# A two-layer image and token network on one core: shared score products, attention output taken by VectorE straight from PSUM, and three quarters of a normalisation moved inside the attention

## Chip, core and metric

The kernel runs on one core of a Trainium2 chip. The metric is device time in microseconds (us). TensorE (PE) multiplies matrices into PSUM, VectorE (DVE) and ScalarE (ACT) work on SBUF and PSUM, GpSimd (POOL) works on SBUF, SyncE (SP) issues the DMAs. Each engine executes its own instruction stream in order and waits on semaphores.

## What is computed

An input `x` of 4 batches x 32 images x 128 x 128 goes through two layers.

```
# layer 0, with x of [4, 32, 128, 128]; _inorm normalises one image
xn = _inorm(xa); k, q, v = three spectral convolutions of xn, 32 heads each
scores = einsum('bntk,bnsk->bnts', qf, kf) / sqrt(Hs*Ws)      # 32 x 32 for each head and batch
p_attn = softmax(scores); av = einsum('bnts,bnsk->bntk', p_attn, vf)
a   = _inorm(p(av) + xa)
m   = two spectral layers of _inorm(a)          # "layer 1" and "layer 2" of the kernel's loops
out = _inorm(m) + a ;  x = x + out
# layer 1: an image row is a token: 4 batches x 4096 tokens of 128
t = x as tokens
q, k, v = _ln_t(t) @ Wq.T, @ Wk.T, @ Wv.T
t = t + softmax(causal(q @ k.T) / sqrt(128)) @ v
t = t + expert layer of _ln_t(t) (64 experts, top 8 tokens each)
```

In the kernel a batch of the second layer is 32 tiles of 128 tokens (4096 tokens), 4 batches, 128 tiles in all.

## The kernel before

**Score products (layer 0).** The scores of the image attention are computed in the frequency domain, as a complex product with three real products in place of four. A product is a tile of 128 modes x (16 heads x 128 images): DVE multiplies modes of the images (`XLT`) by a weight of each head (`CT`) into one of four buffers `ZP`, PE contracts it into the score banks with 4 matmuls (8 in the trace). There are 2 halves of the heads x 5 mode tiles x 3 products = 30, in `score_products` (L1037), all on DVE, both inputs in SBUF. PE's matmul is L1344. Afterwards DVE adds and subtracts a maximum (L1711 to L1715), ACT takes the exponential (L1469), DVE goes on. ACT's stream is in order: ahead of the exponential stand 128 row-wise activations of the image (L1466), and a load of its function table.

**Value products.** 36 x 3 products, DVE (L981, one input in PSUM) with POOL beside it (L993).

**End of layer 0.** `_inorm(m) + a`, in 32 groups of 4 images. Of each four groups ACT normalises three (L1545) and DVE one (L1911); POOL adds the result to `U` (`x1_ready`, L1183); DVE takes the statistics for the token normalisation (L1773). Then all 128 coefficients are computed (`row_moments`, `token_norm`; ready at L773, `norm_ready`), and the attention starts. The weights of the token layer are prepared ahead of it by DVE (`fold_weights`, L741 to L755) and PE (L373 to L375).

**The attention of layer 1** is written out in slots, one for each of 288 units (72 a batch; a unit is two key tiles of 128 by a query group of up to 512). In slot s PE computes the scores of unit s (`scores`, 2 x 3 matmuls), weighs the values with unit s-2 (`weigh`, 2 x 3 matmuls), and computes up to three pieces of the row maxima for a later group (`top_scores`, L433). ACT takes two exponentials per unit (L654 in f32, L657 in f16; `ex_ev`, `hi_ev`), DVE the difference of the two (L827, both inputs in SBUF; `lo_ev`) and the maxima (L807). Score banks are double buffered, the f16 halves threefold.

At most one job a slot uses the spare bank, PSUM bank 7: `kt` (turn tokens), `qp` (project queries), `m` (turn maxima) and `out` (apply the value weights to the sums of a finished group; two halves a group, in adjacent slots mostly). Before a job PE waits in `spare_bank` until the job ahead of it has emptied the bank (`kt_ev`, `ql_ev`, `ml_ev`, `os_ev`). `attention_plan` sets jobs to slots by due times.

An `out` job is finished by three engines: ACT copies the bank into `OTM` (L690, `os_ev`), DVE takes the reciprocals of the sums (L839), POOL scales (2 x L622) and adds to `U` (L625, `or_ready`), DVE takes statistics three slots later (L846). POOL also prepares the tokens of the next batch, 8 chunks a batch (`prep_slot`, L609 to L612), and DVE splits them (`split_low`, L798).

## Time and profile before

| | before |
|---|---|
| median of 3 runs | 2064.22 us (2062.46 to 2067.7) |
| profiled execution, own time | 2063.2 us |
| its span in the trace | 2061.3 us |
| PE / DVE / ACT / POOL busy | 84% / 76% / 51% / 24% |
| score products | 124.25 to 190.4 us |
| end of layer 0 to coefficients ready | 799.15 to 855.66 us |
| attention with its start | 855.7 to about 1819.7 us |

The span runs from the first to the last instruction; times in the trace count from its start. A share of busy time is a mean over stages with different limits. A wait is read from an instruction's idle time and its releaser.

### The profile page before, as it was taken

How to read it: one execution, taken by the hardware profiler on the slowest of the kernel's cores; microseconds unless marked ns; L12 is line 12 of the kernel's file. 1: busy time of each engine (PE TensorE's matmuls, PEld its weight loads, DVE VectorE, ACT ScalarE, POOL GpSimd, SP SyncE). 2: the span in 40 equal slices, each digit the busy share in tenths (PEclk: the TensorE clock that was granted, in tenths of full speed). 3: DMA queues.
4: the chain of work that ended last, by engine and by line, in shares of the span. 5: the costliest groups of instructions: out<-in, count | busy, mean ns of one | idle time of the engine just before them, and what ended most of it. 6: DMA issues, size and time to landing. Idle time of an engine off the chain costs nothing.

```text
span 2061.3 us, 31131 instructions
## 1 busy us (share of the span) xinstructions
PE 1729.3 (84%) x11530; PEld 1076.7 (52%) x11530; DVE 1569.2 (76%) x3012; ACT 1059.8 (51%) x1632; POOL 491.8 (24%) x591
## 2 busy tenths in 40 slices
PE   8765777899789993189999899998999999966767
PEld 8631222699789893044444444454444544434535
DVE  5789999538766689789887888778886888578345
ACT  5396000133545246356677667776667777772110
POOL 2200666100190073524200541125200311000000
PEclk9886999999899996589999999999999999998878
DMA  6550353000000050001000110001000000030686
GB/s 171 203 148 11 85 127 76 1 1 1 1 1 1 1 170 1 3 8 24 11 1 1 21 21 1 1 1 32 11 1 1 1 1 1 1 123 1 216 306 172
DMA packets 113683, 101.00 MB, mean 49 GB/s; under 512 B 39168, under 2 KB 91776, under 8 KB 112992
## 3 DMA queue, kind: packets, MB, share of 16 engines
q1 hardware_dynamic: 113536, 99.02, 17.0%
q8 instruction: 95, 1.56, 0.3%
q14 instruction: 52, 0.43, 0.1%
HBM read 80.27 MB, written 12.44 MB: 45 GB/s over the span
## 4 chain that ended last, share of the span: by engine, by line
PE 62%; DVE 23%; issue 6%; ACT 3%; DMA 3%; POOL 2%; SPq 1%; POOLq 0%; DVEq 0%; ACTq 0%
PE PS L451 5%; PE PS L453 5%; PE PS L452 5%; PE PS L470 5%; PE PS L472 5%; PE PS L471 5%; PE PS L1269 4%; DVE U L981 4%; PE PS L1278 4%; PE PS L433 4%; DVE U L1037 3%; PE PS L1196 3%; PE PS L1402 3%; DMA V<-in_L_ffn_weight 3%; DVE ST L1773 2%
## 5 line engine op out<-in xcount | busy, mean ns | idle before, releaser
L827 DVE TENSOR_TENSOR DB<-Z 128x1024 f16<-128x1024 f32 (+2 forms) x288 | 335.2, 1164 | 117.6 <-ACT Z L657 69.0
L654 ACT ACTIVATE Z<-PS,MI 128x1024 f32<-128x1024 f32 (+2 forms) x288 | 300.5, 1043 | 240.8 <-PE PS L453 206.8
L807 DVE TENSOR_REDUCE MI<-PS 128x1 f32<-128x512 f32 (+2 forms) x576 | 357.5, 639 | 47.7 <-PE PS L433 31.3
L657 ACT ACTIVATE Z<-PS,MI 128x1024 f16<-128x1024 f32 (+2 forms) x288 | 298.7, 1037 | 0.0
L622 POOL TENSOR_SCALAR Z<-Z,MI 128x128 f32<-128x128 f32 x128 | 89.1, 707 | 699.6 <-DVE MI L839 699.6
L981 DVE TENSOR_TENSOR U<-A,PS 128x1408 f32<-128x1408 f32 x108 | 166.1, 1615 | 1.2 <-PE PS L1368 1.2
L993 POOL TENSOR_TENSOR U<-A,U 128x1408 f32<-128x1408 f32 x36 | 113.9, 3196 | 192.0 <-DVE MI L1734 137.7
L1374 PE MATMUL PS<-U 128*32 128x352 f32 x1152 | 110.7, 480 | 0.1
L470 PE MATMUL PS<-Z,A 128*128 128x512 f16 (+3 forms) x288 | 104.0, 361 | 4.3 <-ACT CST L665 4.0
L470 PE MATMUL PS<-Z,V 128*128 128x512 f16 (+3 forms) x288 | 104.0, 361 | 3.8 <-ACT CST L665 3.6
L1269 PE MATMUL PS<-CST,A 128*66 128x128 f32 x768 | 104.8, 281 | 0.5 <-DVE A L1769 0.5
L451 PE MATMUL PS<-V 128*128 128x512 f16 (+3 forms) x288 | 104.6, 363 | 0.0
L453 PE MATMUL PS<-V 128*128 128x512 f16 (+3 forms) x288 | 104.5, 363 | 0.0
L452 PE MATMUL PS<-V 128*128 128x512 f16 (+3 forms) x288 | 104.5, 363 | 0.0
L451 PE MATMUL PS<-A,V 128*128 128x512 f16 (+3 forms) x288 | 104.2, 362 | 0.0
L453 PE MATMUL PS<-A,V 128*128 128x512 f16 (+3 forms) x288 | 104.0, 361 | 0.0
L471 PE MATMUL PS<-DB,V 128*128 128x512 f16 (+3 forms) x288 | 104.0, 361 | 0.0
L452 PE MATMUL PS<-A,V 128*128 128x512 f16 (+3 forms) x288 | 104.0, 361 | 0.0
L471 PE MATMUL PS<-DB,A 128*128 128x512 f16 (+3 forms) x288 | 104.0, 361 | 0.0
L472 PE MATMUL PS<-Z,V 128*128 128x512 f16 (+3 forms) x288 | 103.9, 361 | 0.0
L472 PE MATMUL PS<-Z,A 128*128 128x512 f16 (+3 forms) x288 | 103.9, 361 | 0.0
L1278 PE MATMUL PS<-CST,DB 66*128 66x128 f32 x768 | 100.6, 275 | 0.1
(412 smaller groups left out, 3710.2 us busy)
## 6 DMA issues: line engine op xcount, KB each, us to landing
V<-in_L_ffn_weight SPq DMA_DIRECT2D x32, 1024.0 KB, 7.6
A<-x_planes SPq DMA_DIRECT2D x24, 528.0 KB, 9.7
U<-in_x SPq DMA_DIRECT2D x16, 512.0 KB, 3.8
V<-in_x SPq DMA_DIRECT2D x4, 2048.0 KB, 13.9
Z<-in_x SPq DMA_DIRECT2D x16, 512.0 KB, 3.9
out<-U SPq DMA_DIRECT2D x16, 512.0 KB, 5.0
U<-e_planes SPq DMA_DIRECT2D x48, 132.0 KB, 7.2
x_planes<-Z SPq DMA_DIRECT2D x2, 1056.0 KB, 8.0
```

Source lines behind the costliest of these rows:

```text
L451: pe.matmul(o, kh[:, ks], qh[:, qs], start=True, stop=False)
L452: pe.matmul(o, kh[:, ks], ql[:, qs], start=False, stop=False)
L453: mm = pe.matmul(o, kl[:, ks], qh[:, qs], start=False, stop=k < 4 * g)
L470: pe.matmul(o, xh[:, k, :], ph, start=k == 0, stop=False)
L471: pe.matmul(o, xh[:, k, :], pl, start=False, stop=False)
L472: mm = pe.matmul(o, xl[:, k, :], ph, start=False, stop=k == 4 * g + 3)
L654: act.activation(EX32[u % 2][:, 0:w], s, ACT.Exp, scale=SCALE / (QUP * KUP), bias=pb).then_inc(sem("ex_ev"), 1)
L657: act.activation(EHI[u % 3][:, 0:w], s, ACT.Exp, scale=SCALE / (QUP * KUP), bias=pb).then_inc(sem("hi_ev"), 1)
L807: dve.tensor_reduce(bm[:, g % 2, t, k:k + 1], PS[:, 4 + chunk_no[c] % 2, 0:w], AX.X, ALU.max).then_inc(sem("ch_ev"), 1)
L827: dve.tensor_tensor(ELO[u % 3][:, 0:w], EX32[u % 2][:, 0:w], EHI[u % 3][:, 0:w], ALU.subtract).then_inc(sem("lo_ev"), 1)
L981: dve.tensor_tensor(YB[d % 2][:, :, q, :], XR[:, r % 2, :, q, :], PS[:, 6 + i % 2, 0:MR].unsqueeze(1).broadcast_to([128, B, MR]), ALU.mult ...
L1269: mm = pe.matmul(PS[0:66, ROW_BANKS[k % 3], 128 * j:128 * j + 128], A_modes[:, :, 4 * k + j], cst["ih"], start=True, stop=True)
```

## The change

1. **Score products.** Of the three products the third goes to POOL (`pool_score_products`, 10 products, two buffers `ZPP` in `Z`), the other two stay on DVE (20). DVE now reads the modes from PSUM, where PE's transposes have put them (`turned`), and the sum of real and imaginary part is accumulated there by 10 more matmuls in place of two DVE adds. The products no longer wait for the Gram matrix except the third (its buffer is read by it).
2. **Attention output.** DVE finishes an `out` job alone from PSUM: reciprocals and two `scalar_tensor_tensor` that scale and add to `U`. ACT's copy, POOL's three instructions and `OTM` are gone. `os_ev` is now given by DVE.
3. **End of layer 0.** Only groups 0 to 7 (batch 0) are normalised ahead of the attention, 6 by ACT and 2 by DVE. Groups 8 to 31 are done in the slots 2, 4, ..., 48 of batch 0: even groups by ACT, odd by POOL, all added by POOL. DVE takes their statistics in the slots 3 to 17 (batch 1), 60 to 67 (batch 2), 132 to 139 (batch 3), and the coefficients of a batch are computed in the slots 20, 70, 142 (`NORM_AT`) and the one behind each. The preparation of batch 1 and its `qp` jobs move later (slots 22 to 43 and 52 to 62), and buffers change places so that the images are not overwritten.
4. **Weights of the token layer** are prepared inside the inverse loop of layer 2: `fold_weights` at step 6, PE's part at step 12 (`token_weights`), `take_weights` at step 18.

```diff
+STATS_AT = {1: 3, 2: 60, 3: 132}
+NORM_AT = {1: 20, 2: 70, 3: 142}
...
         def prep_slot(b, c):
-            return UB * (b - 1) + 3 + 3 * c if b else slots.start + 3 * (c // 2)
+            return UB * (b - 1) + (3, 22)[b == 1] + 3 * c if b else slots.start + 3 * (c // 2)
+
+        def image_slot(g):
+            return 2 * (g - 7)
+
+        def by_pool(g):
+            return g >= 8 and g % 2 == 1
+
+        def by_dve(g):
+            return g in (2, 5)
...
-            def add_out(job):
-                _, b, g, h = job
-                n = kind_no[job]
-                pool.wait_ge(sem("os_ev"), n + 1)
-                pool.wait_ge(sem("rd_ready"), n + 1)
-                x = OTM[n % 2][:, :, 0:128]
-                for j in range(2):
-                    ins = pool.tensor_scalar(x[:, j], x[:, j], rd[:, n % 2, j:j + 1], None, ALU.mult)
-                pool_steps.later(ins)
-                u = U[:, NT * b + 4 * g + 2 * h:NT * b + 4 * g + 2 * h + 2, :]
-                pool.tensor_tensor(u, u, x, ALU.add).then_inc(sem("or_ready"), 1)
...
-                        act.activation(OTM[n % 2], PS[:, 7, :].rearrange("p (j d) -> p j d", j=2)[:, :, 0:130], ACT.Copy).then_inc(sem("os_ev"), 1)
...
+                for g in range(8, NIM):
+                    if image_slot(g) == s and not by_pool(g):
+                        last_norm(act, g)
+                for b in range(1, B):
+                    if NORM_AT[b] == s:
+                        root_tokens(b)
...
                 elif kind == "out":
                     n = kind_no[job]
-                    dve.wait_ge(sem("os_ev"), n + 1)
-                    dve.reciprocal(rd[:, n % 2, :], OTM[n % 2][:, :, 128]).then_inc(sem("rd_ready"), 1)
+                    dve.wait_ge(sem("out_mm"), n + 1)
+                    later(dve.reciprocal(rd[:, n % 2, :], PS[:, 7, 128:385:256]))
+                    for j in range(2):
+                        u = U[:, NT * b + 4 * x + 2 * y + j, :]
+                        ins = dve.scalar_tensor_tensor(u, PS[:, 7, 256 * j:256 * j + 128], rd[:, n % 2, j:j + 1], u, ALU.mult, ALU.add)
+                    ins.then_inc(sem("os_ev"), 1)
...
+                for b in range(1, B):
+                    if 0 <= s - STATS_AT[b] < 16 and (s - STATS_AT[b]) % (2 if b == 1 else 1) == 0 and (b == 1 or s - STATS_AT[b] < 8):
+                        g = 8 * b + (s - STATS_AT[b]) // (2 if b == 1 else 1)
+                        dve.wait_ge(sem("x1_ready"), g + 1)
+                        image_stats(U, g).then_inc(sem("st_ready"), 1)
+                    if NORM_AT[b] == s:
+                        dve.wait_ge(sem("st_ready"), 8 * b)
+                        token_variance(slice(NT * b, NT * b + NT))
+                    if NORM_AT[b] + 1 == s:
+                        batch_norm(b)
...
-            eng.tensor_tensor(ZP[z % 4][0:w], XLT[0:w, xc, k, :].unsqueeze(1).broadcast_to([w, 16, N]),
-                              CT[0:w, wc, k, 16 * h:16 * h + 16].unsqueeze(2).broadcast_to([w, 16, N]),
+            dve.tensor_tensor(ZP[n % 4][0:w], turned(2 - c, k, w).unsqueeze(1).broadcast_to([w, 16, N]),
+                              CT[0:w, c, k, 16 * h:16 * h + 16].unsqueeze(2).broadcast_to([w, 16, N]),
                               ALU.mult).then_inc(sem("zp_dve"), 1)
+
+        def pool_score_products(pool, i):
+            h, k = divmod(i, NLC)
+            w = min(128, ML - 128 * k)
+            if i >= 2:
+                pool.wait_ge(sem("s_mm"), 3 * (i - 1))
+            pool.tensor_tensor(ZPP[i % 2][0:w], XLT[0:w, 0, k, :].unsqueeze(1).broadcast_to([w, 16, N]),
+                               CT[0:w, 2, k, 16 * h:16 * h + 16].unsqueeze(2).broadcast_to([w, 16, N]),
+                               ALU.mult).then_inc(sem("zp_pool"), 1)
...
+            pool.wait_ge(sem("xlt_ev"), 1)
+            pool.wait_ge(sem("x_out"), 48)
+            for i in range(2 * NLC):
+                pool_score_products(pool, i)
```

VectorE in the slots 75 and 76, the start of batch 1, before: `L827` is the difference of the halves, `L807` a row maximum, `L839` the reciprocal of an `out` job, which waits for ACT's copy (`os_ev`), `L798` the split of a prepared chunk, which waits for POOL (`xh_pool`).

```order
L807 TENSOR_REDUCE MI<-PS 128x1 [waits ch_mm]
L839 RECIPROCAL MI<-Z 128x2 [waits os_ev]
L807 TENSOR_REDUCE MI<-PS 128x1 [waits ch_mm]
L827 TENSOR_TENSOR DB<-Z 128x1024 [waits pv_mm,hi_ev,ex_ev]
L807 TENSOR_REDUCE MI<-PS 128x1 [waits ch_mm]
L839 RECIPROCAL MI<-Z 128x2 [waits os_ev]
L807 TENSOR_REDUCE MI<-PS 128x1 [waits ch_mm] x2
L798 TENSOR_TENSOR V<-Z,V 128x512 [waits xh_pool]
L827 TENSOR_TENSOR DB<-Z 128x896 [waits pv_mm,hi_ev,ex_ev]
```

The same place of VectorE after the change (`L857` is the maximum, `L877` the difference, `L889` and `L892` the `out` job, `L848` the split):

```order
L857 TENSOR_REDUCE MI<-PS 128x1 [waits ch_mm]
L889 RECIPROCAL MI<-PS 128x2 [waits out_mm]
L892 SCALAR_TENSOR_TENSOR U<-PS,MI,U 128x128 [waits dve_step]
L892 SCALAR_TENSOR_TENSOR U<-PS,MI,U 128x128
L857 TENSOR_REDUCE MI<-PS 128x1 [waits ch_mm]
L877 TENSOR_TENSOR DB<-Z 128x1024 [waits pv_mm,hi_ev,ex_ev]
L857 TENSOR_REDUCE MI<-PS 128x1 [waits ch_mm]
L889 RECIPROCAL MI<-PS 128x2 [waits out_mm]
L892 SCALAR_TENSOR_TENSOR U<-PS,MI,U 128x128 [waits dve_step]
L892 SCALAR_TENSOR_TENSOR U<-PS,MI,U 128x128
L857 TENSOR_REDUCE MI<-PS 128x1 [waits ch_mm] x2
L848 TENSOR_TENSOR A<-Z,A 128x512 [waits xh_pool]
```

One reciprocal a job has become a reciprocal, a wait for it, and two more instructions, in front of the next maximum.

ScalarE in the slots 19 to 21 of batch 0 after the change (`L691` and `L694` are the exponentials of a unit, `L676` the root of a batch's variances, `L702` the copy of a group's sums):

```order
L691 ACTIVATE Z<-PS,MI 128x1024 [waits lo_ev,st_mm]
L694 ACTIVATE Z<-PS,MI 128x1024 [waits pv_mm]
L676 ACT_TABLE_LOAD
L676 ACTIVATE MI<-MI 128x32 [waits var_ready]
L691 ACT_TABLE_LOAD [waits lo_ev]
L691 ACTIVATE Z<-PS,MI 128x1024 [waits st_mm]
L694 ACTIVATE Z<-PS,MI 128x1024 [waits pv_mm]
L702 ACTIVATE CST<-PS 128x512 [waits out_mm,pv_mm]
```

A root with a load of the function table on either side now stands between two units; the root waits for VectorE. It stands in the slots 20, 70 and 142. Before, no root and no table load stood between the first and the last exponential.

## Rows read from the trace of the kernel before

**Rows 1.** The page: busy time of each engine over the span
```profile
PE 1729.3 (84%) x11530; PEld 1076.7 (52%) x11530; DVE 1569.2 (76%) x3012; ACT 1059.8 (51%) x1632; POOL 491.8 (24%) x591
```

**Rows 2.** Windows by stage: length, PE, PEld, DVE, ACT, POOL busy, clock, DMA
```profile
124.00:190.00 66.00, 42.41 (x232) 5.15 (x232) 65.94 (x31) 61.62 (x113) 0.00 (x0) 0.77 0.23 48
...
803.00:856.00 53.00, 0.00 (x0) 0.00 (x0) 52.08 (x181) 33.52 (x88) 38.05 (x32) 0.50 0.00 0
...
880.00:1100.00 220.00, 208.31 (x1132) 103.62 (x1132) 180.22 (x300) 150.61 (x172) 53.18 (x90) 0.97 0.05 11
...
1140.00:1373.00 233.00, 223.71 (x1227) 112.24 (x1226) 187.33 (x305) 162.85 (x185) 58.39 (x96) 1.00 0.06 10
...
1606.00:1815.00 209.00, 204.75 (x1105) 102.83 (x1102) 157.01 (x246) 150.87 (x169) 34.79 (x48) 1.00 0.00 1
```

**Rows 3.** Timeline of 95 to 205 us: start, length, engine, line [idle before <-releaser]
```profile
115.22 69.12 ACT L1466 ACTIVATE V<-V,MI 128x128 f32<-128x128 f32 x128
116.94 3.76 SPq L1113 DMA_DIRECT2D A<-x_planes  x8
124.25 66.14 DVE L1037 TENSOR_TENSOR U<-U,MI 128x2048 f32<-128x2048 f32 x30
126.69 1.93 PE L1344 MATMUL PS<-U 128*32 128x512 f32 x8 [3.61 <-DVE U L1037]
...
184.36 1.28 ACT L1469 ACT_TABLE_LOAD   x1
190.45 1.93 PE L1344 MATMUL PS<-U 32*32 32x512 f32 x8 [0.27 <-DVE U L1037]
195.02 1.22 DVE L1715 TENSOR_TENSOR U<-U,MI 128x1024 f32<-128x1024 f32 x1
196.28 1.06 ACT L1469 ACTIVATE U<-U 128x1024 f32<-128x1024 f32 x1 [10.64 <-DVE U L1715]
```

**Rows 4.** Groups by line: shapes xcount | busy us, mean ns | idle before
```profile
L827 DVE TENSOR_TENSOR DB<-Z 128x1024 f16<-128x1024 f32 (+2 forms) x288 | 335.2, 1164 | 117.6 <-ACT Z L657 69.0 <-issue 43.3 <-PE PS L472 3.1
...
L981 DVE TENSOR_TENSOR U<-A,PS 128x1408 f32<-128x1408 f32 x108 | 166.1, 1615 | 1.2 <-PE PS L1368 1.2
...
L1853 DVE SCALAR_TENSOR_TENSOR A<-PS,MI,A 128x128 f32<-128x128 f32 x66 | 22.6, 342 | 3.7 <-ACT A L1489 3.5
```

**Rows 5.** One line each: shortest/median/longest ns, first and last start
```profile
L993 POOL TENSOR_TENSOR U<-A,U x36: 3168/3196/3213, 206.2 to 371.2; 128x1408 f32<-128x1408 f32 x36
L622 POOL TENSOR_SCALAR Z<-Z,MI x128: 597/602/1916, 917.8 to 1817.8; 128x128 f32<-128x128 f32 x128
```

**Rows 6.** Timeline of 728 to 856 us, layer 2's loop and layer 0's end
```profile
748.05 0.75 DVE L1882 SCALAR_TENSOR_TENSOR V<-V,MI,PS 128x512 f32<-128x512 f32 x1 [0.28 <-PE PS L1278]
...
799.15 37.06 ACT L1545 ACTIVATE V<-V,MI 128x128 f32<-128x128 f32 x96 [1.99 <-DVE MI L1904]
800.94 1.26 POOL L1183 TENSOR_TENSOR U<-U,V 128x512 f32<-128x512 f32 x1 [28.18 <-ACT V L1545]
803.77 0.21 DVE L755 CAST MI<-CST 128x128 bf16<-128x128 f32 x1
...
844.98 4.72 DVE L1773 BATCH_NORM_STATS2 ST<-U 128x6 f32<-128x128 f32 x24
855.43 0.23 DVE L773 TENSOR_SCALAR Z<-Z 128x128 f32<-128x128 f32 x1
```

**Rows 7.** Timeline of POOL and DVE at the start of batches 1 and 2
```profile
1141.94 1.18 POOL L622 TENSOR_SCALAR Z<-Z,MI 128x128 f32<-128x128 f32 x2 [44.16 <-DVE MI L839]
1374.78 1.18 POOL L622 TENSOR_SCALAR Z<-Z,MI 128x128 f32<-128x128 f32 x2 [44.17 <-DVE MI L839]
...
1143.18 1.23 DVE L827 TENSOR_TENSOR DB<-Z 128x1024 f16<-128x1024 f32 x1 [0.82 <-issue]
1170.18 0.69 DVE L798 TENSOR_TENSOR V<-Z,V 128x512 f16<-128x512 f32 x1 [2.29 <-POOL V L612]
```

**Rows 8.** Timeline of ACT at the first exponential; PE and DVE at the last `out` job
```profile
894.62 1.28 ACT L654 ACT_TABLE_LOAD   x1
896.46 1.01 ACT L654 ACTIVATE Z<-PS,MI 128x896 f32<-128x896 f32 x1 [0.56 <-PE PS L455]
...
1819.20 0.49 DVE L846 BATCH_NORM_STATS2 ST<-U 128x6 f32<-128x128 f32 x2 [1.44 <-POOL U L625]
```

More of the change, by code:

```diff
@@ L1905, in _ @@
             dve.wait_ge(sem("fin_coef"), 1)
-            dve.wait_ge(sem("a_kept"), 1)
-            fold_weights(dve, later)
-            for g in range(NIM + 5):
-                if g < NIM and g % 4 == 3:
+            for g in range(8):
+                if by_dve(g):
                     for i in range(4 * g, 4 * g + 4):
```

185 lines of the change are left out of this document (115 added, 70 removed).

## Prediction

> **What bounds the kernel now.** I read the page first, then a table of windows by stage, then the timelines of the places that the change touches. The page gives PE 84% and DVE 76% of the span [rows 1], but that is a mean over stages with different limits. By stage [rows 2]: the score products keep DVE busy for 65.94 of 66 us; the end of layer 0 keeps DVE busy for 52.08 of 53 us, with PE at nothing; in the attention PE is busy for 223.71 of 233 us in batch 1 and 204.75 of 209 in batch 3, where nothing is prepared for a next batch, while DVE has 187.33 of 233. So two short stages are bound by DVE, and the long one by PE. The attention has about 9 us of idle PE in each of the batches 1 and 2, 12 us in the stretch shown of batch 0 and 4 in batch 3: some 35 us are all that it can win.
>
> **Score products.** POOL can start about when the modes have been copied, and `x_out` is already through, since SP issues the loads behind it at 116.94 [rows 3]. I let all start at 124.25, the old start, at the latest. POOL: 10 products of 2048 columns. Its nearest row is L993, 3196 ns for 1408 columns [rows 5], so 2048 x 2.27 = 4.65 us each, 46.5 us: done at 170.8. DVE: 20 products with one input in PSUM, as L981: 1615 ns for 1408 [rows 4], so 2.35 us each, 47 us: done at 171.3. PE: 30 steps of at most 1.93 us (a step takes that at the low clock; the granted clock of the stage is 0.77, between the levels of 1.2 and 2.4 GHz) [rows 2, 3], 58 us: done at 182.2 at worst. Behind the last matmul (190.45 + 1.93 = 192.4) DVE needs until 195.02 + 1.22 = 196.24, thus 3.9 us, before ACT's exponential [rows 3]. It would be ready between 171.3 + 1.9 + 3.9 = 177 and 186 us, 10 to 19 us earlier.
>
> But ACT is late next. Its 128 activations run from 115.22 to 184.34, the table load behind them ends at 185.64, and the exponential follows in the same stream. Before, ACT waited 10.64 us there [rows 3]. The edit does not touch that work. So the stage gives back 196.28 - 185.64 = **10.6 us**, and up to 9 us of DVE's and POOL's gain is lost in ACT's queue. Bounds: 10.2 (PE always at the low clock) to 10.6. The ten added matmuls and five copies lie ahead of 124.25, beside the Gram matrix that was waited for.
>
> Would POOL and DVE block each other? The 36 instructions of L993 lie between 3168 and 3213 ns, though DVE works all the time beside them with one input in SBUF and one in PSUM [rows 5, 4]. That is the form that the products now have, so I add nothing.
>
> **End of layer 0.** Before: ACT starts at 799.15, the coefficients are ready at 855.43 + 0.23 = 855.66 [rows 6]. After: ACT has 6 groups of 4 activations, at 37.06 / 96 = 0.386 us each 9.3 us; POOL adds 8 groups, the first at 800.94, at about 1.24 us each (1.26 in the row), which ends at 810.9 and is the longer chain. The statistics of the last group take 4 x 4.72 / 24 = 0.8 us: 811.7. The coefficients took from 849.7 to 855.66, 6.0 us, on 128 columns [rows 6]; for 32 columns I take 4.0 (they are 17 dependent steps; bounds 3 and 6). Ready at 815.7, **40.0 us** earlier (bounds 38 and 41). The start of the attention behind it (to the first exponential at 896.46, [rows 8]) keeps its steps, some 41 us.
>
> **Weights of the token layer.** From 799.15 to 803.77 + 0.21 DVE and PE took 4.8 us [rows 6]; that was beside ACT's work and POOL's adds and gives nothing. In the loop of layer 2 it goes onto PE's chain: PE's four f32 matmuls and transposes, about 0.6 to 1 us, stand on the path; DVE's 3 to 3.5 us lie in its waits of 0.28 us a step, four in five steps [rows 6], fourteen steps of which follow the second piece. **+1.0 us**, bounds 0 and 3.5 (nothing hidden).
>
> **Attention.** Five effects, per slot of 233 / 72 = 3.24 us (the same POOL instruction comes at 1141.94 and 1374.78 [rows 7]).
> - *Output on DVE.* Each of 64 jobs adds two instructions like L1853 (342 ns) and a wait for the reciprocal, about 0.85 us [rows 4]: 14 us a batch, DVE to 201 of 233 [rows 2]. PE stays the bound, but bank 7 is now held until DVE, behind its difference and a maximum, has finished, where ACT's copy freed it at once. The second job of a pair is due one slot later. By my count, an estimate, scores end half-way into a slot (1.6 us); two exponentials take some 2.1 (1.01 for 896 columns [rows 8]), the difference 1.16 [rows 4], a maximum 0.6, the job 0.85: 6.3 us, and PE is there after two slots, 6.5. It is just in time; I take 0.1 us for 32 pairs, **+3** (bounds 0 and 20).
> - *POOL's part gone.* DVE's split of a chunk waits up to 2.29 us for POOL, which has `out` jobs ahead of it [rows 7]; and differences wait 43.3 us in all with no releaser shown [rows 4], one of them 0.82 us, until POOL's L622 was over (1141.94 + 1.18, start at 1143.18 [rows 7]). These go. But at the start of a batch DVE has six jobs in twelve slots, 5 us more, and takes the bound over in part. I take half of PE's idle time in the batches 1 and 2, 3.5 us each, and 1 us in the others: **-8** (bounds -16 and -3).
> - *Images in batch 0.* 24 groups: DVE 0.8 us each; ACT 12 x 1.55 us; POOL 24 adds of 1.26 us and 12 x 4 scalings. ACT has 150.61 of 220 us and hides its part. DVE's eight in the slots 3 to 17 stand where it is densest (three maxima a slot), and wait for ACT's group and POOL's add of the same slot, some 0.6 us each; the others are 0.8 us on each of eight slots in a row. 180.22 of 220 is the mean [rows 2]. I take 4 of the first 6.4 us as lost, 2 of the other 13: **+6** (bounds 2 and 15). The `qp` jobs of batch 1 move to slots without maxima, **-1**.
> - *Coefficients in the slots 20, 70, 142.* DVE gets 11 dependent small steps (about 2.4 us) and 4 more a slot later. ACT's root waits for the first, with a table load of 1.28 us on each side [rows 8]. The load ahead of it is hidden by the wait; the load behind it and the wait delay the next exponentials by about 2.5 us in slot 20. Scores and weights are buffered for about that long; in the slots 70 and 142, which are short for PE (2.6 us), it is not enough. 1 + 2.5 + 2.5 = **+6** (bounds 2 and 12).
> - *Tail.* The last job passes ACT, DVE, POOL, DVE, its last statistics start at 1819.20 [rows 8]; two engines drop out: **-2** (bounds -1 and -4).
>
> Sum of the attention: 3 - 8 + 6 - 1 + 6 - 2 = **+4 us**.
>
> ScalarE: Activation LUTs (the Trainium skill, section "What ACT_TABLE_LOAD costs") puts a switch at 1.28 us for the load and 1.38 for a drain. Here the exponential stood ready 0.56 us behind the end of a load, released by PE [rows 8], so that at most 0.56 us can be a drain. By the page three switches back would cost another 4 us: the attention +8, the time 2023, inside the forecast's own range; I give it 1 in 10 of that.
>
> **Sum.** -10.6 - 40.0 + 1.0 + 4 = -45.6 us. The profiled execution took 2063.2 us (a span of 2061.3 and 1.9 around it), the median of the runs 2064.2, 1 us more. From the median: **2018.6 us**, its own range 2008 to 2030.
>
> **Rivals.**
> - *The spare bank binds.* If DVE runs later than in my count, every `out` job holds bank 7 longer. For: only 0.2 us of room a pair. Against: DVE has 32 us a batch left. At 0.6 us for each of the 32 pairs it is 19 us in place of 3: 2035.
> - *VectorE and GpSimd block each other less.* Only 20 us of POOL's work is left in each of the batches 1 and 2 and none in batch 3, so that DVE's 43.3 us of unexplained waits vanish [rows 4] and PE wins most of its idle time there. The attention gives back 12 us in place of +4: 2003. Against: PE waits little for these differences; L622 itself ran up to 1916 ns where 597 is its shortest [rows 5], so often DVE won. SBUF — State Buffer (the Trainium skill, "Who interferes with whom") says that a VectorE instruction with two SBUF inputs and a GpSimd one that reads SBUF exclude each other for a whole instruction. By that rule batch 0 loses instead: POOL reads there for 52 us where it read for 36, and 1.26 us adds stand in front of the differences.
> - *Batch 0 is overfull.* DVE's statistics, waiting for ACT and POOL in the dense slots, push PE: all of 19 us of statistics and the small steps come on top, 25 in place of 12: 2032.
> - *Slower than before.* The mechanism is bank 7 with DVE a whole slot behind: a job then waits for a difference, two maxima and the job, 2.6 us, at 32 pairs and as many single jobs behind them: 64 x 2.6 = 166 us in place of 3, 2182 us. It decides from 49 / 64 = 0.8 us a job on. DVE would have to be full; it is at 201 of 233.
>
> **How the numbers follow.** Forecast 0.66; bank or batch 0, 2030 to 2045, 0.17; the attention gains, 2000 to 2008, 0.12; slower 0.02; 0.03 for a score stage or an end of layer 0 that gives half. The range of 8 in 10 leaves out little more than the far end of both: 2004 to 2035. A measurement of this kernel can tell about 0.3%, 6 us. Faster 0.96, same 0.02, slower 0.02.
>
> **What would show it.** The exponential of the scores at about 185.6 us with no idle time ahead of it; coefficients of batch 0 ready some 40 us behind the start of what is 799.15 now less 10, namely 16 to 17 us after it; attention, from there to the last statistics, about as long as the 964 us now, plus 4. A longer wait of PE's `out` matmuls for DVE, or of scores for exponentials at the slots 20, 70 and 142, tells where it went wrong. The prediction is wrong by more than its range only if POOL's products take over 6 us each, or the attention changes by over 15.

## The result, and the profile after

The changed kernel takes **2038.7 us** (median of 4 runs, 2036.3 to 2044.9); the kernel before took 2066.0 us in the same comparison (2062.5 to 2068.9). The ratio is 0.987, interval 0.985 to 0.990. It is faster, clear of noise, but by 27 us (1.3%) where 45.6 (2.2%) were forecast, and 3.7 us above the end of the range. The spans of the two profiled executions differ by 24.9 us (2061.3 and 2036.4), and the ledger below is made on them.

The page of after, to be held against [rows 1]:

```profile
PE 1734.1 (85%) x11550; PEld 1086.7 (53%) x11550; DVE 1574.0 (77%) x3154; ACT 1038.2 (51%) x1553; POOL 435.0 (21%) x457
```

It tells nothing of the missing 18 us; the stages do. First the scores, in the timeline of after (start, length, engine, line, idle time and releaser in brackets), to be held against [rows 3]:

```profile
119.75 11.56 ACT L1560 ACTIVATE V<-V,MI 128x128 f32<-128x128 f32 x21
121.12 7.18 POOL L1113 TENSOR_TENSOR Z<-U,MI 128x2048 f32<-128x2048 f32 x2 [52.27 <-DVE U L1791]
...
171.80 1.23 DVE L1803 TENSOR_TENSOR U<-U,MI 128x1024 f32<-128x1024 f32 x1
186.39 1.28 ACT L1563 ACT_TABLE_LOAD   x1
187.68 1.06 ACT L1563 ACTIVATE U<-U 128x1024 f32<-128x1024 f32 x1
188.77 1.22 DVE L1805 TENSOR_REDUCE MI<-U 128x32 f32<-128x1024 f32 x1 [15.74 <-ACT U L1563]
```

ACT's exponential has no idle time ahead of it any more, and DVE, which used to be late, has been ready since 173.0 us and waits 15.7 for it. The exponential comes 8.6 us earlier, 10.5 if one takes off that ACT began its 128 activations 1.85 us later in this execution (117.07, before 115.22).

The loop of layer 2, the same view:

```profile
728.43 27.83 POOL L1253 TENSOR_TENSOR U<-U,Z 128x1024 f32<-128x1024 f32 x12
734.86 0.60 DVE L778 COPY MI<-Z 128x3 f32<-128x3 f32 x1
735.03 1.08 PE L1344 MATMUL PS<-CST,A 128*66 128x128 f32 x8
735.50 6.94 DVE L780 TENSOR_SCALAR Z<-Z,MI 128x128 f32<-128x128 f32 x3
735.95 1.06 PE L1353 MATMUL PS<-CST,DB 66*128 66x128 f32 x8
743.53 2.08 PE L1353 MATMUL PS<-CST,DB 66*128 66x128 f32 x8 [5.61 <-DVE DB L1962]
```

And its windows (length, then busy us of PE, PEld, DVE, ACT, POOL; granted clock; DMA share and GB/s):

```profile
735.50:743.60 8.10, 2.50 (x23) 2.31 (x21) 8.10 (x9) 2.26 (x8) 8.10 (x4) 0.76 0.75 221
743.60:750.00 6.40, 6.40 (x30) 6.40 (x31) 5.11 (x18) 1.13 (x4) 6.40 (x4) 0.51 0.82 238
750.00:764.00 14.00, 14.00 (x124) 13.77 (x123) 11.96 (x43) 5.79 (x21) 13.27 (x6) 1.00 0.52 154
```

Three scalings of 128 columns take 6.94 us, each the length of one of POOL's additions (27.83 / 12 = 2.3 us). Each scaling ends 0.1 us behind one of these additions. PE waits 5.6 us for what DVE does behind them, and comes back at the lower of its two levels (clock 0.51, the group of eight matmuls 2.08 us, not 1.06) for some 6 us. DVE's scalings with an input in PSUM (`L1962`, 0.33 us each, from 742.36) ran beside the next addition without a wait. From the reciprocal ahead of the loop (730.2, after 722.8) to ACT's first scaling behind it (799.15, after 801.34) it was 69.0 us and is now 78.6: **+9.6 us** where the prediction had +1.0.

The end of layer 0, to be held against [rows 6]:

```profile
801.34 9.34 ACT L669 ACTIVATE V<-V,MI 128x128 f32<-128x128 f32 x24 [2.00 <-DVE MI L1997]
803.12 1.32 POOL L626 TENSOR_TENSOR U<-U,V 128x512 f32<-128x512 f32 x1 [39.47 <-ACT V L669]
813.24 0.87 DVE L1861 BATCH_NORM_STATS2 ST<-U 128x6 f32<-128x128 f32 x4 [0.35 <-POOL U L626]
...
817.78 0.18 DVE L820 TENSOR_SCALAR Z<-Z 128x32 f32<-128x32 f32 x1
```

Coefficients 16.6 us after the start (forecast: 16 to 17). To the first exponential it is 56.85 us where it was 97.31: -40.5.

The attention, from the first to the last exponential; rows of ACT's first exponential in each batch and of the last one:

```profile
858.19 1.01 ACT L691 ACTIVATE Z<-PS,MI 128x896 f32<-128x896 f32 x1 [0.29 <-PE PS L477]
1109.75 1.01 ACT L691 ACTIVATE Z<-PS,MI 128x896 f32<-128x896 f32 x1
1343.71 1.01 ACT L691 ACTIVATE Z<-PS,MI 128x896 f32<-128x896 f32 x1
1574.86 1.01 ACT L691 ACTIVATE Z<-PS,MI 128x896 f32<-128x896 f32 x1 [2.16 <-PE PS L477]
1787.93 0.58 ACT L691 ACTIVATE Z<-PS,MI 128x384 f32<-128x384 f32 x1
```

That is 929.7 us; before it was 913.5 (896.46 to 1809.98). **+16.2 us**, 15.4 of it in batch 0 (251.6, before 236.2). One place of it, the slots 70 and 71, in the timeline:

```profile
1103.45 1.28 ACT L676 ACT_TABLE_LOAD   x1
1104.51 0.21 DVE L1868 TENSOR_TENSOR MI<-ST 128x32 f32<-128x32 f32 x1
...
1106.84 0.18 DVE L806 TENSOR_SCALAR MI<-MI 128x32 f32<-128x32 f32 x1
1106.95 1.09 DVE L877 TENSOR_TENSOR DB<-Z 128x896 f16<-128x896 f32 x1
1107.06 0.23 ACT L676 ACTIVATE MI<-MI 128x32 f32<-128x32 f32 x1 [2.33 <-DVE MI L806]
1107.31 1.28 ACT L691 ACT_TABLE_LOAD   x1
1107.96 1.28 DVE L857 TENSOR_REDUCE MI<-PS 128x1 f32<-128x512 f32 x2
1108.60 0.58 ACT L691 ACTIVATE Z<-PS,MI 128x384 f32<-128x384 f32 x1
1108.79 0.38 PE L455 MATMUL PS<-V 128*128 128x512 f16 x1 [2.49 <-DVE MI L857]
```

Eleven dependent steps keep DVE from 1104.51 to 1107.02. Behind them stand the difference and a maximum, and PE waits 2.49 us for the maximum. ACT meanwhile waits 2.33 us between its two loads. The two slots take 8.23 us, before 5.82.

In slot 20 one of the same steps meets an image addition of POOL:

```profile
932.43 1.26 POOL L626 TENSOR_TENSOR U<-U,V 128x512 f32<-128x512 f32 x1
932.59 1.14 DVE L1869 TENSOR_SCALAR MI<-MI 128x32 f32<-128x32 f32 x1
```

It took 1.14 us, in the slots 70 and 142 0.18. PE waited 2.7 us there, in no_images, where the step took 0.18, 1.7.

A second effect came with these waits: TensorE's granted clock fell, in the attention, where it had stayed at 1.00 before (windows of after, columns as above):

```profile
937.60:944.40 6.80, 6.12 (x17) 2.64 (x18) 5.08 (x9) 5.93 (x9) 4.29 (x7) 0.50 0.00 0
1343.80:1347.20 3.40, 3.40 (x17) 1.53 (x16) 3.02 (x6) 1.95 (x3) 0.00 (x0) 0.50 0.00 0
```

The first stretch begins at the end of the wait in slot 20, the second 1.1 us behind the one in slot 142; an f16 matmul of 512 columns takes 0.63 us in them, 0.38 outside. The price can be read from kernels that have the same wait in slot 142 with such a stretch behind it or without: the slots 0 to 5 of batch 2 take 20.53 us in after and 18.95 in no_stats, 1.6 us for 3.4 us at the lower level. The first stretch then costs some 3.0 us (an estimate from the same price), both together 4.6 of the 16.2.

The ledger of the span: start-up +1.85, scores -10.45, value stage to layer 2 +1.2, loop of layer 2 +9.6, end of layer 0 -40.5, attention +16.2, behind the last exponential -2.8: together -24.9.

### The profile page after: what moved, and what is told of

It is laid out like the page before. It is cut to its first block, busy times and chain, and to the rows that moved or that the text cites. A ratio compares the mean times of both kernels' runs of the same rounds, so it can differ in the third digit from the quotient of the medians.

```text
span 2036.4 us, 30968 instructions
## 1 busy us (share of the span) xinstructions
PE 1734.1 (85%) x11550; PEld 1086.7 (53%) x11550; DVE 1574.0 (77%) x3154; ACT 1038.2 (51%) x1553; POOL 435.0 (21%) x457
## 4 chain that ended last, share of the span: by engine, by line
PE 64%; DVE 16%; ACT 8%; issue 6%; DMA 3%; SPq 1%; POOL 1%; DVEq 0%; ACTq 0%
PE PS L473 5%; PE PS L475 5%; PE PS L474 5%; PE PS L492 5%; PE PS L494 5%; PE PS L493 5%; PE PS L1271 4%; PE PS L1344 4%; PE PS L1353 4%; PE PS L455 4%; DVE U L1046 4%; ACT V L1560 3%; PE PS L1496 3%; DMA V<-in_L_ffn_weight 3%; ACT Z L694 2%
## 5 line engine op out<-in xcount | busy, mean ns | idle before, releaser
L691 ACT ACTIVATE Z<-PS,MI 128x1024 f32<-128x1024 f32 (+2 forms) x288 | 300.3, 1043 | 256.0 <-PE PS L475 221.0
L877 DVE TENSOR_TENSOR DB<-Z 128x1024 f16<-128x1024 f32 (+2 forms) x288 | 332.1, 1153 | 96.8 <-ACT Z L694 52.8
L857 DVE TENSOR_REDUCE MI<-PS 128x1 f32<-128x512 f32 (+2 forms) x576 | 356.7, 639 | 39.2 <-PE PS L455 22.7
L694 ACT ACTIVATE Z<-PS,MI 128x1024 f16<-128x1024 f32 (+2 forms) x288 | 298.6, 1037 | 0.0
L652 POOL TENSOR_SCALAR Z<-U,Z 128x128 f32<-128x128 f32 x104 | 65.5, 643 | 360.5 <-PE PS L494 243.0
L473 PE MATMUL PS<-V,A 128*128 128x512 f16 (+3 forms) x288 | 105.0, 365 | 0.0
L475 PE MATMUL PS<-V,A 128*128 128x512 f16 (+3 forms) x288 | 104.7, 364 | 0.0
L474 PE MATMUL PS<-V,A 128*128 128x512 f16 (+3 forms) x288 | 104.7, 364 | 0.0
```

The lines of the kernel that those rows point to most:

```text
L473: pe.matmul(o, kh[:, ks], qh[:, qs], start=True, stop=False)
L474: pe.matmul(o, kh[:, ks], ql[:, qs], start=False, stop=False)
L475: mm = pe.matmul(o, kl[:, ks], qh[:, qs], start=False, stop=k < 4 * g)
L691: act.activation(EX32[u % 2][:, 0:w], s, ACT.Exp, scale=SCALE / (QUP * KUP), bias=pb).then_inc(sem("ex_ev"), 1)
L694: act.activation(EHI[u % 3][:, 0:w], s, ACT.Exp, scale=SCALE / (QUP * KUP), bias=pb).then_inc(sem("hi_ev"), 1)
L857: dve.tensor_reduce(bm[:, g % 2, t, k:k + 1], PS[:, 4 + chunk_no[c] % 2, 0:w], AX.X, ALU.max).then_inc(sem("ch_ev"), 1)
```

## The experiments

In the attention two executions of the same code agree nearly everywhere to 0.1 us a stretch of six slots, so that one profile shows what the whole time can't. The exceptions are the places behind PE's waits for the coefficients, by the length of the stretch at the lower clock: the slots 18 to 23 of batch 0 take 23.85 us in after, 23.68 in exp_ahead and 22.33 in fold_late, which have the same attention. "Attention" below is the time from the first exponential to the last, "batch 0" that between the first exponentials of the batches 0 and 1, "low" the time in the attention with a granted clock of 0.5.

| kernel | attention | batch 0 | batches 1, 2, 3 | low |
|---|---|---|---|---|
| before | 913.5 | 236.2 | 232.8, 233.5, 211.0 | 0 |
| after | 929.7 | 251.6 | 234.0, 231.2, 213.1 | 6.8 + 3.4 |
| exp_ahead | 930.0 | 251.6 | 234.2, 231.1, 213.1 | 6.8 + 3.4 |
| fold_late | 928.0 | 249.8 | 234.7, 230.4, 213.1 | 3.4 + 3.4 |
| old_out | 939.0 | 255.3 | 238.8, 233.8, 211.1 | 3.4 + 3.4 + 3.4 |
| root_late | 927.5 | 250.3 | 234.0, 230.1, 213.1 | 3.4 |
| no_tables | 927.6 | 249.5 | 234.5, 230.8, 212.9 | 3.4 + 3.4 |
| no_stats | 920.5 | 245.9 | 232.0, 229.6, 213.1 | 6.8 |
| no_images | 916.8 | 239.4 | 233.6, 230.8, 213.1 | 3.4 + 3.4 |
| no_coefs | 917.3 | 243.3 | 231.5, 229.5, 212.9 | 0 |
| bare | 906.4 | 234.2 | 229.6, 229.5, 213.1 | 0 |
| one_root | 924.7 | 252.4 | 229.6, 229.6, 213.1 | 3.4 |
| act_only | 923.5 | 251.4 | 229.5, 229.5, 213.1 | 3.4 |
| pool_only | 927.1 | 255.1 | 229.5, 229.5, 212.9 | 6.8 |

**fold_late**: the weights of the token layer later in the loop (the notes behind `#` are added here).

```diff
-                    if layer == 2 and k == 6:    # DVE, fold_weights
+                    if layer == 2 and k == 20:
-                    if layer == 2 and k == 12:   # PE, token_weights
+                    if layer == 2 and k == 26:
-                    if layer == 2 and k == 18:   # DVE, take_weights
+                    if layer == 2 and k == 32:
```

> After, with the weights of the token layer taken later in the loop of layer 2: DVE's first piece at k = 20 in place of 6, PE's four steps at k = 26 in place of 12, DVE's second piece at k = 32 in place of 18. By then POOL has finished the 16 additions that it ran back to back from 726 to 763.7 us. Theory 1 (block): the three 128x128 scalings took 6.94 us in place of 0.68 only because each waited for a whole addition of POOL (2.3 us), and PE then ran for some 6 us at the low clock. They should take about 0.7 us again, and the loop should end 8 to 9 us earlier, at some 793 us in place of 801.3; the whole 2030. Theory 2 (load): DVE and PE have no room in this loop at any place, and the same instructions cost there what they cost now; the loop ends within 2 us of 801.3, or later, since less of the loop is left to catch up: the whole 2037 to 2040. What the prediction had for the edit, +1.0 us against the kernel before, is what is left if theory 1 holds.

2038.9 us (ratio 0.989, 0.987 to 0.992): the whole time shows no gain. The loop takes 74.3 us in place of 78.6, half-way between the two theories. Its timeline says why:

```profile
760.04 3.03 DVE L778 COPY MI<-Z 128x3 f32<-128x3 f32 x1
763.10 0.68 DVE L780 TENSOR_SCALAR Z<-Z,MI 128x128 f32<-128x128 f32 x3
```

Without the stall the loop was quicker, and k = 20 came while POOL was still adding (until 763.04). A copy of three columns then took 3.03 us; the three scalings behind it, with POOL done, 0.68. The granted clock was at 0.5 for 3.4 us of this loop (from 766.7), for 10.2 us of after's. So theory 1 holds for each instruction, and its place was chosen a little too early. The 4.2 us of the loop and 1.8 of the attention don't show in the whole because the time behind the last exponential was 5 us longer in this profile (253.5 us, after 248.5); in kernels with the same code there it lies between 247.9 and 254.5.

**exp_ahead**: the exponential of the scores ahead of ACT's last 24 activations.

```diff
             for w in range(W):
+                if w == 104:
+                    act.wait_ge(sem("once_dve"), MADE["sd"])
+                    act.activation(SE, SD, ACT.Exp).then_inc(sem("se_ready"), 1)
                 ins = act.activation(Vc[:, w, :], Vc[:, w, :], ACT.Identity, scale=rim[:, w:w + 1], bias=cim[:, w:w + 1])
             ins.then_inc(sem("xg_ready"), 1)
-            act.wait_ge(sem("once_dve"), MADE["sd"])
-            act.activation(SE, SD, ACT.Exp).then_inc(sem("se_ready"), 1)
```

> After, with ACT's exponential of the scores ahead of the last 24 of the 128 activations that stand in front of it (0.54 us each). DVE's part of the scores was ready at 173.0 us, ACT's exponential started at 187.7. Theory 1 (ACT is what is late, as the prediction says): the exponential starts at some 174.5 to 176 us, that is 12 to 13 us earlier, and the value products follow. How much of it the end of the value stage keeps is open: PE needs PT, which ACT copies behind the remaining 24 activations (13 us), about at the old time less 0 to 2 us, but DVE's first products start ahead of that. If only the exponential counts, the value stage ends 10 us earlier: 2028. Theory 2 (ACT's queue as a whole is late, whatever its order): PT comes at the old time and the stage ends within 2 us of 370.0: 2037 to 2039.

2032.3 us (ratio 0.985, 0.982 to 0.988).

```profile
175.33 1.06 ACT L1562 ACTIVATE U<-U 128x1024 f32<-128x1024 f32 x1
...
176.42 1.22 DVE L1806 TENSOR_REDUCE MI<-U 128x32 f32<-128x1024 f32 x1 [3.06 <-ACT U L1562]
...
190.11 0.77 PE L1462 MATMUL PS<-Z,ST 96*128 96x352 bf16 x2 [5.03 <-ACT U L1567]
```

The exponential starts at 175.33, 12.3 us earlier than in after, and the reciprocal ahead of layer 2's loop comes 9.9 us earlier (712.9, after 722.8). Theory 1 holds: ACT's queue was late. The whole is 6.4 us shorter, not the 10 of the expectation. The rest of the 12.3 is lost in the same queue, as PE now waits 5.03 us for ACT's copies of PT behind the 24 activations.

**root_late**: variance, root and reciprocal in slots of their own.

```diff
-NORM_AT = {1: 20, 2: 70, 3: 142}
+NORM_AT = {1: 18, 2: 68, 3: 140}
+ROOT_AT = {1: 19, 2: 70, 3: 142}
+READY_AT = {1: 21, 2: 72, 3: 144}
```

> After, with the three sets of coefficients taken apart in time: the variances in the slots 18, 68 and 140, ACT's roots in 19, 70 and 142, the reciprocals in 21, 72 and 144 (now the variance and the root in the same slot, 20, 70 and 142, and the reciprocal one later). Now ACT waits there 1.55 and 2.33 us for DVE between its two table loads, and slot 70 takes 7.08 us where it took 2.6. Theory 1 (the waits cost): the waits go, the two loads of 1.28 us stay; slots 70 and 142 win 1.5 to 2 us each and slot 20 about 2, together 5: 2034. Theory 2 (the loads cost, the waits lay in time that DVE needed anyway): 0 to 1.5 us in all: 2037 to 2039.

2034.7 us (ratio 0.986, 0.983 to 0.989). Read in the attention it is -2.2 us, not the 5 of theory 1, and no more than the clock gives: 3.4 us at the lower level in place of 10.2. The slots 66 to 71 of the batches 0 and 1 win 0.5 us each, and lose as much in the slots 73 and 145, behind the reciprocals. The waits of ACT lay in time that DVE's steps needed anyway; moved two slots ahead, the steps make PE wait there. The only wait of PE around slot 70 in root_late (total us, times, longest):

```profile
PE PS L460 <- DVE MI L859: 1.8, 1, 1.8
```

The root and its two loads stay in slot 70 here, and the slots 70 and 71 take 5.82 us together, as before the change and as in no_coefs: the loads alone cost nothing there.

**old_out**: the output of the attention as before, by ACT, DVE and POOL; all else as in after.

```diff
-                    dve.wait_ge(sem("out_mm"), n + 1)
-                    later(dve.reciprocal(rd[:, n % 2, :], PS[:, 7, 128:385:256]))
...
+                    dve.wait_ge(sem("os_ev"), n + 1)
+                    dve.reciprocal(rd[:, n % 2, :], OTM[n % 2][:, :, 128]).then_inc(sem("rd_ready"), 1)
```

> After, with the output of the attention as it was: ACT copies bank 7, DVE takes the reciprocals, POOL scales and adds; all else as in after. Theory 1 (the prediction): the output on DVE costs 3 us by bank 7 and gives 8 by POOL's part, so that undoing it loses some 5 us, 2 in batch 0 and 3.5 in each of the batches 1 and 2 less what bank 7 gives back: 2044. Theory 2 (bank 7 is the cost): the slots behind a pair of outputs took 0.65 us longer than before in every batch; undone, the attention wins 5 to 10 us: 2029 to 2034. Theory 3: in batch 0, POOL has the images too, and the old way adds its waits there: batch 0, 251.6 us now, takes 255 or more, while the batches 1 to 3 go back to 232.8, 233.5 and 211.

2051.6 us (ratio 0.994, 0.992 to 0.996), 13 us above after; in the attention +9.2. Theory 2 fails; theory 1 has the direction, at not quite twice its 5 us. Theory 3 holds for batch 0 (255.3), batch 2 (233.8) and batch 3 (211.1, as before). It fails for batch 1 (238.8, not 232.8), which has the slow start of before again (42.0 us for the slots 0 to 11, before 41.2, after 38.1) and still the statistics and coefficients at its end. The slot that follows a POOL queue with images and outputs in it shows how; the granted clock is at 0.5 from 990.9 on, for 3.4 us:

```profile
987.57 1.74 DVE L869 TENSOR_TENSOR V<-Z,V 128x512 f16<-128x512 f32 x1 [3.21 <-POOL V L668]
991.61 0.58 PE L455 MATMUL PS<-A,V 128*128 128x512 f16 x1 [4.05 <-DVE MI L878]
```

**one_root**: the edit of exp_ahead; the weights at k = 24, 28 and 32; batch 1's coefficients as in root_late; one root for the batches 2 and 3; their statistics in the slots 46 to 61.

```diff
-STATS_AT = {1: 3, 2: 60, 3: 132}
-NORM_AT = {1: 20, 2: 70, 3: 142}
+STATS_AT = {**{3 + 2 * i: 8 + i for i in range(8)}, **{46 + i: 16 + i for i in range(16)}}
+SETS = {18: (1, 2, 19, 21), 62: (2, 4, 63, 65)}   # variance slot: first batch, end, root slot, reciprocal slot
```

> After with four edits, each read at its own stage. (1) The exponential of the scores as in exp_ahead: it should start at 174 to 176 us again. (2) The weights of the token layer at k = 24, 28 and 32 of the layer-2 loop. In fold_late the first piece (k = 20) still fell on POOL's last additions: a copy of three columns took 3.03 us, and from the reciprocal to ACT's first scaling the loop took 74.3 us (69.0 before, 78.5 in after). If the block is the whole matter, it takes 70 to 71; if the instructions and PE's change of pace cost, 73 to 74. (3) In the attention one root for the batches 2 and 3 together (slot 63; variances in 62, reciprocals in 65) in place of slots 70 and 142; that of batch 1 as in root_late. If the table loads and the steps around them are the 2.9 us that slots 66 to 71 of batch 1 cost more than before, that goes to 0. (4) The statistics of the images of both batches in slots 46 to 61, of which eight have no maxima on DVE, in place of 60 to 67 and 132 to 139. Slots 60 to 65 of batch 0 cost 3.4 us more than before, those of batch 1 1.5. If DVE's queue is what costs, both go and up to 1 us comes at 46 to 53; if an image group costs wherever it stands, batch 0 stays at 250 or more. By the first of each the attention, 929.7 us from the first to the last exponential in after, takes 921 to 924, and the whole 2018 to 2022; by the second 929 and 2028.

**2019.6 us** (ratio 0.976, 0.973 to 0.979), 1 us from what had been forecast for the change, which is a coincidence: it contains the 10 us of exp_ahead, which nobody had forecast. The rows of its loop:

```profile
759.07 0.15 DVE L777 COPY MI<-Z 128x3 f32<-128x3 f32 x1
759.25 0.68 DVE L779 TENSOR_SCALAR Z<-Z,MI 128x128 f32<-128x128 f32 x3
```

The loop takes 71.05 us (714.34 to 785.39), 2.1 more than before: with no stretch at the lower clock: that is what the instructions themselves cost, and 7.5 of the 9.6 us were the block and its consequence. In the batches 1 and 2 the excess of the slots 60 to 71 is gone (229.6 us each). The slots 63 and 64 of batch 0 take 9.58 us where they take 6.75 in no_stats, so this root with its variances costs 2.8 us, and 0.9 more stand in slot 66 behind the reciprocals; but there is now one root less. The statistics cost in their new place too: +1.7 and +0.7 us in the slots 48 to 59, and batch 0 stays at 252.4. The second theory of edit (4) holds.

**no_stats, no_images, no_tables, no_coefs, bare** leave out work of after, as their expectations say; one profile each.

> After, leaving out DVE's statistics of the 24 image groups inside the attention (24 x 0.87 us and their waits for POOL's addition); ACT's and POOL's part of the images, the variances, roots and coefficients stay. Batch 0 takes 251.6 us in after and 236.2 before, batch 1 234.0 and 232.8. The prediction had 6 us for all images in batch 0, mostly for these statistics. If the statistics are the cost, batch 0 falls by 6 to 8 us and slots 60 to 65 of batch 0 by 3.4; if it is ACT's scalings and POOL's additions, by 2 at most.

Attention -9.2 us: batch 0 -5.7, and the rest where the statistics of batch 3 stood and in the slots 0 to 5 of batch 2, where the clock doesn't fall here.

> After, leaving out all work on the 24 image groups inside the attention: ACT's 12 x 4 scalings, POOL's 12 x 4 scalings and 24 additions, DVE's statistics; the variances, roots and coefficients stay. Against no_stats this shows what ACT and POOL cost, against after the whole. What then stays over the kernel before is the output on DVE (bank 7) and the coefficients. If images are the cause of the long batch 0, it falls to 241 to 243 (236.2, and 5 for the two roots); if the output on DVE is, it stays above 246.

Attention -12.9; batch 0 falls to 239.4. Beyond no_stats, 6.5 us of batch 0 go with ACT's and POOL's part (at most 2 expected). 3.0 of them lie in the slots 18 to 23, where no_stats has 6.8 us at the lower clock and no_images none, and 3.0 in the slots 30 to 47. In no_images the clock falls at the starts of the batches 1 and 2 instead, so that over the whole attention only 3.7 us go.

> After, with the three roots inside the attention computed as the identity, so that ACT loads no table there (6 loads of 1.28 us go; the waits, the root's own 0.23 us and all steps on DVE stay). If the loads are the cost of the coefficients, slots 18 to 23 of batch 0 fall by 2, slots 66 to 71 of batch 0 and of batch 1 by 2.5 each: 7 us in all. If DVE's dependent steps are, everything stays within 1.5 us.

Attention -2.1, nearly all in the slots 18 to 29. But fold_late, with all its loads, has -1.8 there, by a stretch at the lower clock of 3.4 us like the one here, not 6.8; against it the loads are worth 0.4 us. The slots 70 and 71 together take 8.24 us, as in after (8.23): without the loads, PE still waits 2.5 us there for DVE's maximum. In slot 70 DVE's steps alone hold the whole length, and in slot 20 nearly so. The second theory holds. By chance this run also shows the block of the loop: POOL paused 0.96 us for a load in the middle of the three scalings:

```profile
734.11 2.73 DVE L780 TENSOR_SCALAR Z<-Z,MI 128x128 f32<-128x128 f32 x3
736.78 0.06 DVE L782 MEMSET MI<- 128x1 f32 x1
737.32 13.95 POOL L1253 TENSOR_TENSOR U<-U,Z 128x1024 f32<-128x1024 f32 x6 [0.96 <-DMA Z<-in_x]
```

They took 2.73 us in place of 6.94, and the loop 75.05 in place of 78.6.

> After, leaving out the coefficients of the batches 1 to 3 inside the attention: no variances, no roots (and so no table loads), no reciprocals; the images with their statistics stay. In no_tables the loads alone were gone and slots 70 and 71 together took 8.24 us as in after (8.23; 5.82 before); in root_late the waits were shorter and they took 7.7. If each of the two, ACT's loads and DVE's chain of dependent steps, is late by itself, only both together give it back: slots 66 to 71 fall by 2.4 to 2.9 us in the batches 0 and 1, slots 18 to 25 of batch 0 by 3, the attention (929.7 us from the first exponential to the last) by about 8. If the slots 70 and 142 are long for another reason, as the output jobs behind them, they stay long.

Attention -12.5: the slots 66 to 71 fall by 2.4 in the batches 0 and 1, the slots 18 to 23 of batch 0 by 5.7 (4.2 against fold_late), the slots 0 to 5 of batch 2 by 1.6. The granted clock stays at 1.00 from the first to the last exponential, as before the change; some 4.6 of the 12.5 us are that.

> After, leaving out both: all work on the 24 image groups inside the attention and the coefficients of the batches 1 to 3. What is left of the change in the attention is the output on DVE and the moved qp jobs. From the first exponential to the last: before 913.5, after 929.7, no_images 916.8. The prediction had +3 for bank 7, -8 for POOL's part and -1 for the qp jobs, thus 907.5 by that (or less 2 where the two batches with a full queue win more). If the output on DVE costs nothing and gives nothing, 913; if it is itself a cost of the long attention, over 914.

Attention 906.4, 7.1 us under before: 1.9, 3.3 and 4.0 us won in the batches 0, 1 and 2, 2.1 lost in batch 3. The clock stays at 1.00 here too. This is the output on DVE with the moved preparation and `qp` jobs of batch 1, by itself.

**act_only, pool_only**: one_root with `by_pool` false for all groups, or true for all from 8 on.

> one_root with ACT scaling all 24 image groups inside the attention (4 activations, 1.64 us, in every second slot from 2 to 48), POOL only adds. In no_images, slots 18 to 47 of batch 0 fell by 6.7 us, in no_stats by 0.1, so that it is ACT's or POOL's part of the images which costs there. Theory A (ACT): a burst of 1.64 us delays the next exponentials, and twelve more bursts cost another 6 us: batch 0, 252.4 us in one_root, takes 257 to 260, the whole 2025. Theory P (POOL): POOL's scalings and additions exclude DVE's differences for a whole instruction, and 48 fewer scalings give it back: batch 0 takes 247 to 250, the whole 2016.

> one_root with POOL scaling all 24 image groups inside the attention (4 scalings, 3.3 us, and an addition of 1.26 us in every second slot of about 6.6 us), ACT none. Theory A (ACT's bursts cost): batch 0, 252.4 us in one_root, takes 246 to 248, the whole 2014. Theory P (POOL's instructions exclude DVE's for their length): 255 to 260, the whole 2024; also POOL, which splits the tokens of batch 1 from slot 22 on beside it, may fall behind and make PE's qp jobs wait from slot 52.

2021.4 us (ratio 0.980, 0.978 to 0.981) and 2023.0 (0.981, 0.978 to 0.984), neither to be told from one_root with certainty. In the profiles batch 0 takes 251.4 and 255.1 us, one_root 252.4. Theory A is refuted (twelve more bursts on ACT cost nothing), and theory P has the direction: 48 scalings fewer on POOL give 1.0 us (2.4 to 5.4 expected), 48 more cost 2.7 (2.6 to 7.6). In pool_only 5.6 us are lost in the slots 30 to 35, where the granted clock is at 0.5 from 961.6 to 968.4, and 2.9 won in the slots 18 to 23, where it doesn't fall in this run.

## Why the prediction was wrong

**Right: the score products.** -10.6 forecast, -10.45 measured from the start of the 128 activations, and exp_ahead shows the named limit (ACT late next). The sizes were kinder than taken (POOL 3.6 us a product, not 4.65), which changed nothing.

**Right: the end of layer 0.** -40.0 forecast, -40.5 measured.

**Wrong: the weights of the token layer, "+1.0 us, bounds 0 and 3.5 (nothing hidden)".** +9.6 measured. The failed step is the bound: it took the 3.5 us of DVE's work as the most that the edit can cost, from rows beside ACT and POOL at the end of layer 0, where POOL's first addition came behind the scalings. It didn't ask what POOL does at the new place: from 726 us on its additions follow each other without a gap. Nor did it ask what a wait of PE does to the granted clock: it had no term for that. The block could have been read from the kernel before, in the rows that the 3.5 us come from. One of two casts of the same size stood beside an addition of POOL and took 1.29 us, the other 0.21:

```profile
802.41 1.36 POOL L1183 TENSOR_TENSOR U<-U,V 128x512 f32<-128x512 f32 x1 [0.21 <-ACT V L1545]
802.56 1.29 DVE L754 CAST MI<-CST 128x128 bf16<-128x128 f32 x1
803.77 0.21 DVE L755 CAST MI<-CST 128x128 bf16<-128x128 f32 x1
```

Of the experiments, fold_late, no_tables and one_root (a copy of 3.03 us; scalings of 6.94, 2.73 and 0.68 us with POOL busy, paused and done) show the cause. 7.5 us are the block with PE's slow return, 2.1 the instructions, and these are inside the bounds. The Trainium skill's page SBUF — State Buffer, section "Who interferes with whom", says that a copy or `tensor_scalar` on VectorE in a two-port mode and a GpSimd instruction exclude each other for a whole instruction. The rows above agree for the scalings, 2.3 us for each; a single instruction can wait longer or less, the copy 3.03 us in fold_late (the rest of one addition, from 760.04 to 760.7, and the whole next one) and 0.60 in after. No row shows in which mode these instructions ran. The prediction had that page on the table for the differences in the attention, not for this edit.

**Right in its sum, by luck in its parts: the output on DVE.** Bank 7 +3, POOL's part -8, the `qp` jobs -1: -6 forecast, -7.1 in bare. The parts were both larger than taken. PE waits 6.1 us for bank 7 in bare (6.8 in after) and showed no such wait before, twice the +3; its waits for DVE's maxima fall from 15.5 us before to 4.3 in bare. A part of the reason falls: the 43.3 us of differences waiting with no releaser [rows 4] were to go with POOL's jobs. In bare, with no `out` job and no image on POOL, they are 44.9:

```profile
L868 DVE TENSOR_TENSOR DB<-Z 128x1024 f16<-128x1024 f32 (+2 forms) x288 | 328.2, 1140 | 105.9 <-ACT Z L691 56.4 <-issue 44.9 <-PE PS L494 3.2
```

What the traces show in its place are DVE's waits for POOL at the split: 17.4 us before, 0.9 in after. The rival "bank 7", 19 us, is excluded at that price: PE waited for it 6.8 us in the whole attention of after, and batch 3, where nothing else changed, lost 2.1.

**Mis-sized: images in batch 0, "+6 (bounds 2 and 15)".** 10.9 us (no_coefs to bare: 917.3 and 906.4, with no low clock in either) to 12.9 (after to no_images), twice the term and inside its bounds. The step "DVE's statistics in the dense slots, some lost" was right for the dense slots, 3.5 us for the 4 taken (slots 0 to 17, after to no_stats). The other 16 groups cost more than the 2 taken: 2.0 in the slots 60 to 71 of batch 0 and 2.0 in those of batch 1. "ACT has 150.61 of 220 us and hides its part" was too kind to ACT and POOL together (3.7 us over the attention). Of the two single causes offered for these, neither was shown to carry it alone.

**Mis-sized: the coefficients, "1 + 2.5 + 2.5 = +6 (bounds 2 and 12)".** 10.4 (bare to no_images) to 12.5 (no_coefs to after). The failed step is what the sum leaves out: it prices the waits and has nothing for the granted clock. In bare, no_coefs and before the clock stays at 1.00 through the attention; in every kernel with these coefficients it falls to 0.5 at least once, for 3.4 to 10.2 us in all (in pool_only at a wait of 3.8 us for an `out` job, in the others at or behind one of 2.5 to 3.4 us for the coefficient steps of DVE; in old_out also at one of 4.05). Without it, at 1.6 us for 3.4, the coefficients cost 7.3 us (bare to no_images) to 7.9 (no_coefs to after), near the forecast. Of single terms, slot 20, "1", measured 2.7 beside no images, with PE's wait of 1.7 us and no fall; beside images 4.2 to 5.7, with POOL's block of 1.0 us and the fall. The slots 70 and 142, 2.5 each, measured 2.4 each and 1.6 behind slot 142 for the clock. Their mechanism was half right: "ACT's root waits, with a table load on each side" did happen, but PE waited for DVE's steps, and taking the loads away won 0.0 us in slot 70 and at most 0.5 in slot 20 (no_tables). Why the clock fell behind some of these waits and not behind others of the same length (2.5 us in slot 70 of after and of no_images) stays open.

The rival "Batch 0 is overfull" has nearly the measured size, 25 us for images and coefficients where it came to 23.3, but not its reason: it took all 19 us of the statistics as lost, and they cost 9.2; the rest came from ACT's and POOL's part, the steps and the clock.

**Right: the tail.** -2 forecast. From the last exponential to the last statistics it is 9.7 us before and 7.8 in after. The other 0.9 of the 2.8 us lie in the layer behind, which takes 240.2 to 246.7 us in kernels with the same code there. Not in the prediction: +1.85 us at the start, ahead of every edit, and +1.2 in the value stage. In the other kernels ACT's 128 activations begin between 115.7 and 117.5 us (before 115.22). Most of the 1.85 is seen in the clock: from the low stretch at the start it comes back to 1.0 at 88.6 us before, at 91.1 in after and between 89.3 and 91.7 in the others. The cause of the 1.2 wasn't looked for; it is 0.5 to 1.35 in the nine kernels with the same code in that stage.

Sum of the errors: weights +8.6, images and coefficients +11.3 (4.6 of it the clock in the attention), start and value stage +3.0, output, tail, scores and layer 0 -2.2: 20.7 us, the difference of the forecast -45.6 and the measured -24.9.

## What to carry to other kernels

A moved instruction has to be priced against what the *other* engines do at its new place: here 3 us of small VectorE work was cheap in one stage and cost 9.6 us in another, because GpSimd ran there without a gap. When a stop of TensorE is added to a stretch in which it is otherwise busy, look at the granted clock behind it too: here that was most of what the coefficients cost beyond their forecast. Look at it also before comparing two traces, since a stretch at the lower level was twice as long in one execution as in another of the same code. When two engines are late at the same place, a run that takes one of them away tells which one holds, if it is read at that slot. Small dependent steps in the queue of a busy engine are not hidden by its mean idle time: what counts is whether the next maximum or difference behind them is one for which the bounding engine waits.
